# Row sums of softmax: taken by ScalarE's accumulator in place of a ones column beside V

## What is computed

```python
q, k, v = (split_heads(x @ W + b) for W, b in ((Wq, bq), (Wk, bk), (Wv, bv)))   # 4 x 16 x 512 x 32
attn = q @ k.T / sqrt(32) + alibi            # alibi = -slope[head] * (511 - key)
attn = where(causal, attn, finfo.min)
p = softmax(attn, axis=-1)
out = p @ v                                  # per head 512 x 32
x = layernorm(x + out @ Wo + bo)
```

## Time and profile before

| | us |
|---|---|
| Median of 3 runs | 1315.18 |
| Lowest and highest | 1308.41, 1316.87 |
| The profiled execution | 1316.87 |
| Its span, first to last instruction | 1315.0 |
| PE, DVE, ACT, POOL busy in it | 1190.7, 800.3, 556.9, 310.7 |

### The profile page before, as it was taken

How to read it: one execution, slowest core, us unless ns; L and a number is a source line. 1 busy time by engine, 2 the same in 40 slices (tenths; PEclk the granted TensorE clock), 3 DMA queues, 4 the chain that set the end, 5 groups by cost and what they waited for, 6 DMA issues and landing times.

```text
span 1315.0 us, 27997 instructions
## 1 busy us (share of the span) xinstructions
PE 1190.7 (91%) x8697; PEld 1074.6 (82%) x8697; DVE 800.3 (61%) x1999; ACT 556.9 (42%) x1341; POOL 310.7 (24%) x458
## 2 busy tenths in 40 slices
PE   5888998999899988579999999999999999999983
PEld 4777887888788776578998899889989998899861
DVE  4667777676767765646556654655566546554675
ACT  3567765675666574043323332323233323232310
POOL 4200200020020020363113311331133113311347
PEclk9999999999999988589999999999999999999975
DMA  8222323232322240162232232122222322232112
GB/s 249 61 59 54 69 69 97 48 71 65 97 49 57 65 121 1 65 178 71 81 82 58 73 89 74 58 73 81 81 58 72 92 71 69 61 96 67 33 41 88
DMA packets 109639, 100.13 MB, mean 76 GB/s; under 512 B 12799, under 2 KB 81791, under 8 KB 109504
## 3 DMA queue, kind: packets, MB, share of 16 engines
q1 hardware_dynamic: 106464, 89.16, 24.9%
q0 software_dynamic: 3040, 9.18, 2.2%
HBM read 64.74 MB, written 9.18 MB: 56 GB/s over the span
## 4 chain that ended last, share of the span: by engine, by line
PE 70%; POOL 7%; DVE 7%; issue 5%; ACT 4%; DMA 3%; SPq 3%; ACTq 0%; POOLq 0%; DVEq 0%
PE bank L762 34%; PE bank L552 12%; PE bank L787 9%; PE bank L678 4%; POOL up_lo L1320 4%; PE bank L661 3%; PE bank L774 2%; SPq L460 2%; DMA up_raw<-in_Wu_dram 2%; PE bank L650 2%; POOL out_dram L1368 2%; DVE scores L1047 1%; PE bank L638 1%; ACT probs L858 1%; DMA q_stack<-qk_hi 1%
## 5 line engine op out<-in xcount | busy, mean ns | idle before, releaser
L762 PE MATMUL bank<-up_hi,xsT_hi 128*128 x1216 | 357.1, 294 | 9.5 <-POOL up_lo L1320 7.7
L762 PE MATMUL bank<-up_hi,xsT_lo 128*128 x1216 | 345.0, 284 | 0.0
L762 PE MATMUL bank<-up_lo,xsT_hi 128*128 x1216 | 344.9, 284 | 0.0
L1320 POOL TENSOR_TENSOR up_lo<-up_raw,up_hi 128x256 fp32r<-128x256 f32 x241 | 169.7, 740 | 487.0 <-ACT up_hi L890 486.8
L1191 DVE SCALAR_TENSOR_TENSOR h_tok<-bank,row_weight,silu 128x128 f32<-128x128 f32 x304 | 93.4, 347 | 303.0 <-ACT silu L948 303.0
L762 PEld LDWEIGHTS bank<-up_hi,xsT_hi 128*128 128x128 f32 x1216 | 233.7, 192 | 15.8 <-issue 15.8
L762 PEld LDWEIGHTS bank<-up_hi,xsT_lo 128*128 128x128 f32 x1216 | 234.3, 193 | 0.0
L762 PEld LDWEIGHTS bank<-up_lo,xsT_hi 128*128 128x128 f32 x1216 | 234.0, 192 | 0.0
L948 ACT ACTIVATE silu<-bank 128x256 f32<-128x256 f32 (+1 forms) x160 | 59.6, 372 | 384.4 <-PE bank L762 384.4
L1208 DVE TENSOR_TENSOR y<-bank,y 128x512 f32<-128x512 f32 x304 | 205.0, 688 | 0.4
L858 ACT ACTIVATE probs<-scores,neg_max 128x512 f32<-128x512 f32 (+3 forms) x256 | 136.5, 557 | 72.2 <-DVE neg_max L1047 71.6
(11 more groups left out here) (155 smaller groups left out, 2124.5 us busy)
## 6 DMA issues: line engine op xcount, KB each, us to landing
up_raw<-in_Wg_dram SPq DMA_DIRECT2D x64, 256.0 KB, 3.1
up_raw<-in_Wu_dram SPq DMA_DIRECT2D x64, 256.0 KB, 4.0
down_raw<-in_Wd_dram SPq DMA_DIRECT2D x64, 256.0 KB, 2.7
k_stack<-qk_hi SPq DMA_DIRECT2D x128, 64.0 KB, 2.0
q_stack<-qk_hi SPq DMA_DIRECT2D x128, 64.0 KB, 2.0
x_tok<-in_x_dram SPq DMA_DIRECT2D x4, 1024.0 KB, 5.8
k_stack<-qk_lo SPq DMA_DIRECT2D x64, 64.0 KB, 2.0
q_stack<-qk_lo SPq DMA_DIRECT2D x64, 64.0 KB, 2.0
```

The costliest lines, as they stand in the source:

```text
L762: mm = pe.matmul(bank[:, n * 2 * P:(n + 1) * 2 * P], a[:, s, k, :], up_w[w][k][:, :, :].rearrange("p a f -> p (a f)")[:, bass.ds(at, 2 * P ...
L1320: pool.tensor_tensor(up_w[1][k][:, e, :], up_raw[:, idx % NUPS, k, :, :].rearrange("p g f -> p (g f)"), up_w[0][k][:, e, :].bitcast(F32), ...
```

## The change

ACT's exponentials write the sum of their row beside `probs`, to `row_sum`, in 4 buffers by head. The ones column goes: `v` of a head has 64 columns, `pvT` 64 partitions, `pv_hi` 128 elements in place of 132. DVE's reciprocal reads `row_sum` and waits for the exponentials of its head; the wait for `pv_hi` moves behind it, ahead of the addition. An exponential that opens a head waits until the reciprocal four heads before is done. POOL no longer waits for the reciprocal, and its 8 copies of ones are gone, with PE's wait for them.

```diff
-VW = 2 * HD + 1
+NRS = 4
...
         q_stack = p1.put("q_stack", [3 * HD, GH, SEQ], F32R)
-        v = p1.put("v", [P, 2, QT, 2 * GH, VW], F32R)
+        v = p1.put("v", [P, 2, QT, 2 * GH, 2 * HD], F32R)
         scores = p1.put("scores", [P, 2, SEQ], F32)
...
         pT_lo = p1.put("pT_lo", [P, 2, SEQ], F32R)
-        pvT = p1.put("pvT", [VW, SEQ], F32)
+        pvT = p1.put("pvT", [2 * HD, SEQ], F32)
         bo_row = p1.put("bo_row", [P, D], F32)
-        pv_hi = p1.put("pv_hi", [P, 2, QT, HD + 1], F32)
+        pv_hi = p1.put("pv_hi", [P, 2, QT, HD], F32)
         pv_sum = p1.put("pv_sum", [P, 2, QT, HD], F32)
...
         neg_max = p1.put("neg_max", [P, 2, QT], F32)
+        row_sum = p1.put("row_sum", [P, NRS, QT], F32)
         row_inv = p1.put("row_inv", [P, 2, QT], F32)
...
                     pe.wait_ge(s_side_dve, done("V", g // 2, 1))
-                if u == 0:
-                    pe.wait_ge(s_vones, 2 * QT)
                 if u % PER_HEAD == 0 and hd >= 2:
...
                         for part in (pT_hi, pT_lo):
-                            mm = pe.matmul(bank[0:VW, i * P:(i + 1) * P], v[:, g // 2 % 2, j, g % 2 * GH + h, :],
+                            mm = pe.matmul(bank[0:2 * HD, i * P:(i + 1) * P], v[:, g // 2 % 2, j, g % 2 * GH + h, :],
                                            part[:, u % 2, at + j * P:at + (j + 1) * P],
...
                 for i in range(QT):
-                    mm = pe.transpose(bank[:, i * VW:(i + 1) * VW], pvT[:, i * P:(i + 1) * P], ident[0:VW, 0:VW])
+                    mm = pe.transpose(bank[:, i * 2 * HD:(i + 1) * 2 * HD], pvT[:, i * P:(i + 1) * P],
+                                      ident[0:2 * HD, 0:2 * HD])
                 mm.then_inc(s_back, 1)
...
                 g, h, tiles = UNITS[u]
+                hd = g * GH + h
                 act.wait_ge(s_biased, u + 1)
...
                     act.wait_ge(s_pT, u - 1)
+                if u % PER_HEAD == 0 and hd >= NRS:
+                    act.wait_ge(s_inv, hd - NRS + 1)
                 for i, at, width in spans(tiles):
                     ex = act.activation(probs[:, u % 2, at:at + width], scores[:, u % 2, at:at + width], ACT.Exp, scale=-1.0,
-                                        bias=neg_max[:, u % 2, i:i + 1])
+                                        bias=neg_max[:, u % 2, i:i + 1], accum_out=row_sum[:, hd % NRS, i:i + 1])
                 ex.then_inc(s_exp, 1)
...
                     act.wait_ge(s_back, hd)
-                act.activation(pvT[:, :], banks[4 + hd % 2][0:VW, :], ACT.Copy).then_inc(s_pvT, 1)
+                act.activation(pvT[:, :], banks[4 + hd % 2][0:2 * HD, :], ACT.Copy).then_inc(s_pvT, 1)
 
             def head_values(hd):
-                parts = banks[4 + hd % 2][:, 0:QT * VW].rearrange("p (i d) -> p i d", i=QT)
+                parts = banks[4 + hd % 2][:, 0:QT * 2 * HD].rearrange("p (i s d) -> p i s d", i=QT, s=2)
                 act.wait_ge(s_back, hd + 1)
...
                     act.wait_ge(s_pvsum, hd - 1)
-                act.activation(pv_hi[:, hd % 2, :, :], parts[:, :, 0:HD + 1], ACT.Copy).then_inc(s_pvhi, 1)
+                act.activation(pv_hi[:, hd % 2, :, :], parts[:, :, 0, :], ACT.Copy).then_inc(s_pvhi, 1)
 
...
                     j = slice(2 * job[2], 2 * job[2] + 2)
-                    lo = dve.tensor_tensor(v[:, t % 2, j, :, HD + 1:VW],
+                    lo = dve.tensor_tensor(v[:, t % 2, j, :, HD:2 * HD],
                                            bank[:, :].rearrange("p (j h d) -> p j h d", j=2, h=2 * GH),
...
             def head_values(hd):
-                parts = banks[4 + hd % 2][:, 0:QT * VW].rearrange("p (i d) -> p i d", i=QT)
-                dve.wait_ge(s_pvhi, hd + 1)
+                parts = banks[4 + hd % 2][:, 0:QT * 2 * HD].rearrange("p (i s d) -> p i s d", i=QT, s=2)
+                dve.wait_ge(s_exp, (hd + 1) * PER_HEAD)
                 if hd >= 2:
                     dve.wait_ge(s_o, hd - 1)
-                dve.reciprocal(row_inv[:, hd % 2, :], pv_hi[:, hd % 2, :, HD]).then_inc(s_inv, 1)
-                dve.tensor_tensor(pv_sum[:, hd % 2, :, :], parts[:, :, HD + 1:VW], pv_hi[:, hd % 2, :, 0:HD],
+                dve.reciprocal(row_inv[:, hd % 2, :], row_sum[:, hd % NRS, :]).then_inc(s_inv, 1)
+                dve.wait_ge(s_pvhi, hd + 1)
+                dve.tensor_tensor(pv_sum[:, hd % 2, :, :], parts[:, :, 1, :], pv_hi[:, hd % 2, :, :],
                                   ALU.add).then_inc(s_pvsum, 1)
...
             pool.memset(hot_pad[:, :, :].bitcast(F32), 0.0).then_inc(s_set, 1)
-            pool.wait_ge(s_set, 1)
-            for n in range(2):
-                for j in range(QT):
-                    pool.tensor_copy(v[:, n, j, :, HD], ones[:, 0:2 * GH]).then_inc(s_vones, 1)
             pool.wait_ge(s_const, 16 * 5)
...
                     pool.wait_ge(s_wlo, len(W_ORDER))
-                pool.wait_ge(s_inv, hd + 1)
                 pool.wait_ge(s_pvsum, hd + 1)
```

More of the change, by code:

```diff
@@ L371, in build @@
         s_o, s_pvT, s_back = semaphore("o_done"), semaphore("pvT_copied"), semaphore("values_transposed")
-        s_inv, s_vones = semaphore("row_inverse_done"), semaphore("ones_column_set")
+        s_inv = semaphore("row_inverse_done")
         s_side, s_side_act, s_side_dve = semaphore("side_done"), semaphore("side_hi_taken"), semaphore("side_taken")
```

## The result

The changed kernel takes 1321.5 us (median of 8 runs, 1318.9 to 1327.8), the kernel before in the same set 1309.5. The ratio is 1.009 with a 95% interval of 1.0066 to 1.0113: slower by about 12 us. The forecast was 1347, 30 us above the 1316.9 that its sum starts from.

A forecast was written before the change was run, and what follows sets the result against it. PE was taken to bound the attention loop, busy 414 of 455 us. 1316.9 + 30 (array shapes) + 3 (ACT reads) - 1 (DVE) - 1 (one column fewer) = 1347.9, stated as 1347 us; range 1307 to 1392.

The forecast's parts named there:

- What bounds the kernel: Attention loop: PE leads, busy 414 of 455 us, 100 us over the next engine, and holds 70% of the span.
- Part 1: ACT exponentials: 256 accumulator reads at 0.083 us, 25 of them on the chain; +3 us, bounds 0 and 13.
- The third rival: Attention loop: reads hold ACT up before `pT_hi`, 99 copies 0.13 us later, PE waits: 13 us, 1330; chance 0.05.
- Part 2: DVE's head sum: the reciprocal runs inside the wait for `pv_hi`, DVE done 6.4 us earlier; -1 us, bounds -6 and 0.
- Part 3: PE's values matmuls and `pvT` transposes: one column fewer, -1 us; 448 array-shape changes at 0.10 us, +30 us.
- The sum: Whole kernel: 1316.9 + 30 + 3 - 1 - 1 = 1347.9, stated as 1347 us.
- The first rival: PE in the attention loop: the array shape costs nothing; 1318 us, no change; chance 0.37.
- the second: PE in the attention loop: each change of array shape costs the whole 0.216 us; 1383 to 1414 us; chance 0.11.
- the fourth: Values matmuls on PE: weight loads hide with the narrower array, 53 ns apart for 60; faster, 1304 us; chance 0.09.

The follow-up runs named there:

- The small copies: Two kernels: a one-element ACT copy behind each exponential, against neither reads nor 64-row transposes; exp_done on the copy 1321.4 us, on the exponential 1320.4 us.
- with neither: The changed kernel with pvT widened by a 65th partition and no accumulator output of the exponentials: 1310.3 us, 0.9978 of the kernel before.

## Why the prediction was wrong, point by point

- **What bounds the kernel** held. PE leads in the loop, the loss is in the loop, and the stretch behind it is as before (792.9 us for 794.2).
- **Part 1, +3 us for the reads, measured +6 to +9.** The price of one came out, 0.083 expected and 0.09 net found, but by luck: the read lasts 188 ns and not 83, and its overlap on both sides makes up for it. The step that failed is the weight: I took the share of the chain that the exponentials hold, 25 of 256. What counts is what stands behind a read in ACT's queue. The earlier trace rows had it: 99 of the 192 `pT_hi` copies began when ACT was busy, and for those a read ahead is a delay for `pT_lo` and the values. The small copies show that occupation alone does it, and PE's idle time for `pT_lo` shows the path: 37.7 us with reads for 32.9 without. The third rival, with 13 us and a chance of 0.05, named this mechanism; it took 0.13 us for each of the 99, and half to two thirds of that came out. Its sign, idle time far above 34 us in the changed kernel, did not come: it is 27.5 us there, and 23.6 in the kernel without reads, so the changes of shape had taken up part of that idle time. How much of the cost goes this way and how much with the lower clock is open.
- **Part 2, -1 us for DVE: nothing measured.** The reciprocal does run inside the wait, but the addition starts out of an idle engine now and takes 292 ns for 261 before (64 x 31 ns = 2 us), and the wait is longer by 4.3 us. The longer wait comes with the reads and the rows: with neither it is 32.9 us. That waits which were expected to be met are met is seen in the reciprocal: no idle time stands ahead of it. That the ones copies of POOL cost nothing was not tested by itself; the kernel with neither, which has none, is level with before.
- **Part 3, +30 us for the array shape: measured +6 to +8.5.** That there is a price for a change of shape, unseen in the diff, was right, and 0.10 us per change is near the 0.12 measured. The step that failed is the count, 448. Of these, 320 change the columns alone and cost nothing; 128 change the rows, into and out of the four transposes of each head. 128 x 0.12 = 15 us, of which 0.4 to 0.57 and not 0.68 reached the end. Rows and columns should have been two terms, each with a lower end of 0.
- The Trainium skill, "TensorEngine Tiling (Array Packing)", says in Key Properties that a change of the tiling mode drains TensorE. For columns the traces do not show it (0.05 us to the next matmul, 0.06 before). For rows there is a delay of 0.12 us, which fits the rule; but the first transpose starts 0.15 us behind a matmul that the trace gives 0.22 us, so that the engine is empty in between is not shown.
- **The sum.** 3 + 30 - 2 was 31; 6 to 9 for the reads and 6 to 8.5 for the rows make 12 to 17, and 12 was found. The forecast for the reads was too small and that for the shapes far too large; that the two errors partly cancel in the total is luck. The first rival (no cost for shapes) is refuted by the kernel without reads, the second (0.216 us each) by the distances, the fourth by the 0.06 us that the values matmuls keep. The third holds in part, as said under part 1.

## What to carry to other kernels

Read the array shape of every matmul out of the built program when an edit takes the contracted dimension from 65 partitions to 64: going down to 64 rows between matmuls of 128 rows cost 0.25 us for every visit here, and a 65th row, left at zero, made it free. Price an instruction added to an engine that is not the bound by what queues behind it, not by its own share of the chain: 23 us of "idle" ACT time cost 6 to 9. A sum that comes along for free in a matmul, as the ones column did, should not be moved to an engine that hands its results to the bound.

## What was not expected of the hardware

- The accumulator read of ACT lasts 188 ns (DVE's 83), though with the overlap on both sides it takes only 0.09 us of the engine. An ACT copy of one element per partition has the same 188 ns and costs the kernel as much.
- A change between 128x128 and 128x64 costs nothing and one between 128x128 and 64x128 costs 0.12 to 0.135 us on the mean. Of the 0.24 us of a visit, 0.09 lie ahead of the four transposes and 0.15 in and behind them. Only transposes have been seen with 64 rows; whether an ordinary matmul pays the same, and what the hardware does in that time, is open.
- No kernel here is faster than the one before. The nearest, with neither cost, leaves out the row sums and is only level with it.
